# Sixteen additions a block that form the Strassen operands T1 to T4 at each change to gate and up: GpSimd instead of VectorE

## The chip, the cores and the metric

The kernel runs on one core of a Trainium2 chip. The time is that of the device in microseconds for one execution, the median of several runs. The engines of the core are TensorE (PE), VectorE (DVE), ScalarE (ACT), GpSimd (POOL) and SyncE (SP); DMAs are issued from the queues of SP, ACT and POOL.

## What is computed

Two residual steps on x of 8 x 256 x 1024 f32. The first adds a linear layer and a conditional difference with a matrix of signs; the second is a gated MLP of width 2752 with adapters of rank 16 picked per batch:

```python
sign = (2 * mask - 1).astype(x.dtype)
x = x + einsum('bsi,oi->bso', x, W) + b + einsum('bsi,bio->bso', x, sign) * coeff[:, None, None]

def lora_add(base, inp, A, B):                 # A, B picked by the batch's index
    t = einsum('bri,bni->bnr', A, inp)
    return base + einsum('bor,bnr->bno', B, t) * 0.5
gate = lora_add(x @ W_gate.T, x, A_gate, B_gate)
up   = lora_add(x @ W_up.T,   x, A_up,   B_up)
act  = silu(gate) * up
x = x + lora_add(act @ W_down.T, act, A_down, B_down)
```

## The kernel before

**Stages.** The eight batches are worked on in two blocks s of four, and a block in two halves of N = 512 columns. A first stage makes x1 (the result of the first step) for both blocks and stores it to `x1_scratch`; it ends at about 201 us. Then each block has its gate and up stage over 22 tiles f of the width, and its down stage. The order in which TensorE goes through the work is written out in `pe_order` (L99), and ScalarE and VectorE follow the same list of events.

**Precision.** Every operand of a matmul is split in a high part (a copy rounded to fp32r, made by ScalarE) and a low part (the operand less its high part, made by VectorE), and each product is three matmuls: high by high, high by low, low by high.

**Strassen.** Gate and up of tiles 1 to 20 are one 2x2 block product by a Strassen-Winograd form of seven products (`PRODUCTS`, L32). Beside the four parts B11, B21, B12 and B22 of x1 it needs T3 = B22 - B12, T2 = B11 + T3, a T1 made from B22 less T2, and T4 = B21 - T2, each for four k of 128 rows: sixteen additions of 128x512 f32 a block (`MADE`, L57). They are made in place in the staging tiles `fx` and `early_x`, in which the parts of x1 have been loaded by SyncE. `form_hi` (L827, ScalarE) and `form_lo` (L1179, VectorE) then round them into `op_b`.

**The order at a change of stage.** Tile 0 is worked by four plain products (events `h`, eight in each half), and between them stand the adapters' A products (events `ta`), which take small tiles `lw` that ScalarE and VectorE split shortly before (`lora_a`); then come the small adapter products `r` (0 and 1, with B_gu) and the Strassen products of tile 1, `g` 1: p1, p5, p6, then `r` 1, p3, p7, p2, the A_down product `td` 0, and p4. `first_tile_steps` (L68) says behind which event ScalarE and VectorE do which step: `a_part` splits adapter tiles, `forms` rounds an operand, `make` makes T3, T2 and T1 of one k, `make4` makes T4, `t sum`, `t own`, `t high` and `t low` treat the A product's result, `lora_b` rounds B_gu, `result` makes a = silu(gate) * up of tile 0. Both engines run these steps strictly in the written order. `form_hi` of T1 to T4 waits for the count `form_t` of makings; `form_make` (L1162) is VectorE's.

**Queues.** GpSimd only issues DMAs (L632 to L786). Behind the last store of x1 it issues the twelve loads of B_gu (`load_b_gu(adapter, 0)`, L723) and the four of A_down (L724). In the loop over blocks it waits until the last adapter tile of the second half is split (L727), issues eighteen loads of the next B_gu (L728) and then stores the operands for the down stage one by one (L740). In block 1 its B_gu and A_down loads have been issued in the down stage of block 0 (L783 to L786). SyncE loads T4's part B21 for k = 2 and 3 when T1 of that k has its low part (L561), since it takes the same staging tile.

Of the kernel before, what the change touches and what calls it, by code (L numbers as in the profile page):

```python
# [67 lines left out]
def first_tile_steps():  # L68

    def a_part(half, *firsts):  # L70
        return [("lw", half, o) for o in firsts]

    def forms(name, *ks):
        return [("form", name, k) for k in ks]

    return {("h", 0, 0): a_part(0, 0, 2) + forms("b12", 1, 2, 3, 0) + forms("b22", 0, 1),
            ("h", 0, 3): forms("b22", 2, 3),
            ("ta", 0, 1): a_part(0, 4) + [("make", 0)],
            ("ta", 0, 3): a_part(0, 6) + [("make", 1)] + forms("t1", 0),
            ("ta", 0, 5): a_part(1, 0) + [("make", 2)] + forms("t1", 1),  # L80
            ("ta", 0, 7): a_part(1, 2) + [("t sum", 0), ("make", 3)] + forms("t1", 2) + [("t own", 0)] + a_part(1, 4)
                          + [("t high", 0), ("t low", 0), ("lora_b", 0)] + forms("t1", 3),
            ("ta", 1, 1): forms("t2", 0, 1, 2, 3) + a_part(1, 6),
            ("r", 0): [("result", 0)],
            ("h", 1, 5): [("make4", 2), ("make4", 3)] + forms("t4", 2, 3),
            ("ta", 1, 7): [("t sum", 1)] + forms("t3", 0),
            ("g", 1, "p1"): [("t own", 1), ("t high", 1), ("t low", 1)] + forms("t3", 1),
            ("g", 1, "p5"): [("lora_b", 1)] + forms("t3", 2, 3) + [("make4", 0), ("make4", 1)],
            ("g", 1, "p6"): forms("t4", 0, 1),
            ("r", 1): [("result", 1)],  # L90
            ("g", 1, "p3"): [("second result",), ("t neg",)]}
# [119 lines left out]
def build(nc, x, mask, coeff, w0, bias, wgu, wgu_half, wd, wd_left, a_gu, a_down, b_gu, b_down, idx, ident, own,  # L211
# [13 lines left out]
    with ExitStack() as ctx:  # L225
# [238 lines left out]
        def lw_use(key):  # L464

            s = key[1]
            return s * (HALVES * KQ + FT) + (key[2] * KQ + key[3] // 2 if key[0] == "ta" else HALVES * KQ + key[2])
# [165 lines left out]
        def _(pool):  # L633
# [50 lines left out]
            def load_b_down(adapter, s, hp):  # L684
                if hp > 1:
                    pool.wait_ge(lo_ready, at["l", s, 2 * hp - 3] + 1)
                for q in range(2):
                    for b in range(4):
# [2 lines left out]
                                       b_down[ds(adapter[b], 1), :, 2 * P * hp:2 * P * (hp + 1)].rearrange(  # L691
                                           "a r n -> (a r) n")).then_inc(bd_loaded[hp % 2], 16)

            def load_operand(s, seg, u):
                name = MOVING[u]
                for kp in range(SEGK):
                    at_op = opd_at(seg, name, kp, 0)
                    pool.dma_start(op_d[:, at_op:at_op + 2, :].rearrange("p a n -> p (a n)"),  # L698
                                   ops_d[s, seg * SEGK + kp, STORED[name], :, :]
                                   ).then_inc(opd_loaded[opd_sem(seg, name, kp)], 16)  # L700
# [23 lines left out]
            load_a_down(adapter)  # L724
            for s in range(BLOCKS):

                pool.wait_ge(lw_l, lw_use(("ta", s, HALVES - 1, HT - 1)) + 1)  # L727
                load_b_gu(adapter, 1)  # L728
                for kp in range(KP):
# [400 lines left out]
        def _(dve):  # L1130
# [28 lines left out]
                cols = slice(h * N, (h + 1) * N)  # L1159
                sub(xs[s][:, 2 * k + 1, cols], src, xs[s][:, 2 * k, cols]).then_inc(xl_ready, 1)  # L1160

            def form_make(s, name, k):  # L1162
                out = fx_ap(later_cell(name, k))
                t2_ap = fx_ap(later_cell("t2", k))
                if name == "t3":
                    dve.wait_ge(form_l, form_count(s, "b22", k))
                    end = sub(out, fx_ap(STAGED["b22", k]), out)
                elif name == "t2":
                    dve.wait_ge(fx_loaded[STAGED["t2", k]], 16 * fx_turn[s, "later", "t2", k])
                    dve.wait_ge(form_t, made_count(s, "t3", k))  # L1170
                    end = add(out, fx_ap(later_cell("t3", k)), out)
                else:
                    if name == "t4":
                        dve.wait_ge(fx_loaded[STAGED["t4", k]], 16 * fx_turn[s, "later", "t4", k])
                    dve.wait_ge(form_t, made_count(s, "t2", k))
                    end = sub(out, out, t2_ap)
                end.then_inc(form_t, 1)

            def form_lo(s, name, k):  # L1179
                dve.wait_ge(form_h, form_count(s, name, k))  # L1180
                sub(op_b[:, op_at(name, k, 1), :], form_src(name, k), op_b[:, op_at(name, k, 0), :]).then_inc(form_l, 1)
# [91 lines left out]
            def first_result(s, half):  # L1273
                if half:
                    dve.wait_ge(form_l, form_count(s, "t3", KQ - 1))
                dve.wait_ge(pe_done, done["r", s, half])
                dve.wait_ge(silu_made, silu_count(s, 0, half))
                mult(a32[:, half, :], (g1, g2)[half][:, :], first_bank(1, half)[:, :]).then_inc(a_made, 1)
                operand_lo((s, 0, ("b11", "b12")[half]), a32[:, half, :])
                if half:  # L1280
                    dve.wait_ge(a_made, a_count(s, 0, 1))
                    sub(t_sum[:, :], a32[:, 1, :], a32[:, 0, :]).then_inc(tm, 1)
# [164 lines left out]
            for key in plan.events:  # L1447
# [17 lines left out]
                for kind, *args in steps_after.get((key[0], *key[2:]), ()):  # L1465
# [2 lines left out]
                        continue  # L1468
                    elif kind == "form":
                        form_lo(s, *args)  # L1470
                    elif kind == "make":
                        for name in ("t3", "t2", "t1"):
                            form_make(s, name, *args)
                    elif kind == "make4":
                        form_make(s, "t4", *args)
                    elif kind == "lw":
                        lora_a(("ta", s, *args))
                    elif kind == "lora_b":
# [290 lines left out]
```

## Time and profile before

| | |
|---|---|
| median of 3 runs | 1579.45 us (1579.41 to 1581.66) |
| span of the profiled execution | 1579.3 us |
| stretches with TensorE always busy | 262 to 660 us, for one |
| the two changes to gate and up | about 201 to 257 us and 889 to 946 us |
| granted TensorE clock, mean | 0.995 of full |
| DMA queues of GpSimd, of SyncE | 33.4% and 26.0% of the 16 DMA engines' span |

PE is the matmul part of TensorE, PEld its weight loads, which overlap; two matmuls that follow each other overlap in the records. A line of the timeline gives the start, the time to the end of the last of "x" instructions, and in brackets the idle time of the engine before it and what ended it. L1132, L1135 and L1138 are VectorE's helpers for subtracting, adding and multiplying, L791 is ScalarE's copy, L1509 and L1505 are TensorE's helpers, so the tile names tell what a step is.

### The profile page before, as it was taken

To read this page: it belongs to the slowest core of one execution; us is meant where nothing else is said; L and a number is where in the kernel's file an instruction comes from. 1 tells how busy PE (TensorE), PEld (TensorE's weight loads), DVE (VectorE), ACT (ScalarE), POOL (GpSimd) and SP (SyncE) were. 2 spreads that over 40 slices of the span, in tenths; PEclk is the share of its full clock that TensorE was granted. 3 is DMA by queue.
4 is the path that set the end of the run, shared out by engine and by line. 5 is a ranking of instruction groups with operands and counts; after the bars stand their busy time and mean duration, and the time that the engine had idled before them with its cause. 6 is when DMAs were issued, how large, how long until landed. Compare 5 with 4: busy or idle time off the path is not lost.

```text
span 1579.3 us, 23432 instructions
## 1 busy us (share of the span) xinstructions
PE 1545.1 (98%) x7550; PEld 1304.1 (83%) x7550; DVE 1220.1 (77%) x2136; ACT 802.3 (51%) x1478; POOL 426.1 (27%) x821
## 2 busy tenths in 40 slices
PE   6999998999999999999999989999999999999999
PEld 6999986888888888878888868888888888778887
DVE  8999887676666677688888887767766667798886
ACT  8999855444444444443334464444444444443332
POOL 0000142333333333253410024332323233443100
PEclk9999999999999999999999999999999999999999
DMA  9999854444444444699593725444444445996653
GB/s 372 374 361 376 322 172 127 147 137 154 144 139 155 156 157 153 230 334 312 168 375 111 241 78 168 157 139 134 148 152 148 131 157 179 316 374 220 216 196 116
DMA packets 141961, 325.66 MB, mean 206 GB/s; under 512 B 22416, under 2 KB 50320, under 8 KB 141840
## 3 DMA queue, kind: packets, MB, share of 16 engines
q0 software_dynamic: 61216, 176.21, 33.4%
q1 hardware_dynamic: 76016, 139.57, 26.0%
q10 hardware_dynamic: 4608, 8.39, 1.4%
q8 instruction: 61, 1.00, 0.3%
q14 instruction: 60, 0.49, 0.1%
HBM read 233.51 MB, written 90.18 MB: 205 GB/s over the span
## 4 chain that ended last, share of the span: by engine, by line
PE 87%; DVE 7%; issue 2%; ACT 2%; DMA 1%; SPq 1%; ACTq 0%; POOL 0%; DVEq 0%
PE ps L1509 59%; PE ps L1505 26%; PE ps L1645 2%; DVE m_raw L1135 1%; DVE m_lo L1132 1%; DVE op_b L1132 1%; DMA acc<-x_scratch 1%; DVE acc L1135 1%; DMA m_raw<-in_mask 1%; DVE lo L1132 1%; ACT hi L791 0%; DVE fx L1132 0%; SPq L512 0%; DVE raw L1132 0%; DVE act_t L1306 0%
## 5 line engine op out<-in xcount | busy, mean ns | idle before, releaser
L1509 PE MATMUL ps<-op_b,hi 128*128 128x512 f32 x1616 | 503.4, 393 | 9.3 <-DVE u L1135 5.6
L1132 DVE TENSOR_TENSOR lo<-raw,hi 128x512 fp32r<-128x512 f32 (+2 forms) x640 | 333.4, 530 | 128.7 <-ACT hi L791 126.7
L791 ACT ACTIVATE hi<-raw 128x512 fp32r<-128x512 f32 (+1 forms) x592 | 304.9, 519 | 220.9 <-PE ps L1509 182.9
L1509 PEld LDWEIGHTS ps<-op_b,hi 128*128 128x128 f32 x1616 | 306.0, 190 | 74.1 <-DVE u L1135 6.4
L1509 PE MATMUL ps<-op_b,lo 128*128 128x512 f32 x808 | 318.0, 394 | 0.0
L1509 PE MATMUL ps<-op_d,hi 128*128 128x512 f32 x800 | 248.5, 392 | 4.4 <-DVE acc L1135 4.1
L1505 PE MATMUL ps<-op_b,hi 128*128 128x512 f32 x816 | 252.0, 390 | 0.0
L638 POOL DMA_DIRECT2D operand_scratch<-ot x140 | 75.3, 541 | 552.4 <-DVE ot L1132 536.1
L1135 DVE TENSOR_TENSOR acc<-acc,ps 128x512 f32<-128x512 f32 x248 | 169.9, 685 | 51.0 <-PE ps L1509 43.3
L1509 PEld LDWEIGHTS ps<-op_d,hi 128*128 128x128 f32 x800 | 147.8, 188 | 39.8 <-DVE acc L1135 9.8
L1505 PEld LDWEIGHTS ps<-op_b,hi 128*128 128x128 f32 x816 | 153.4, 188 | 30.7
L1509 PEld LDWEIGHTS ps<-op_b,lo 128*128 128x128 f32 x808 | 153.5, 190 | 29.7
L1505 PE MATMUL ps<-op_b,lo 128*128 128x512 f32 x408 | 159.1, 390 | 0.0
L1509 PE MATMUL ps<-op_d,lo 128*128 128x512 f32 x400 | 156.2, 391 | 0.0
L1132 DVE TENSOR_TENSOR raw<-raw 128x512 f32<-128x512 f32 (+1 forms) x240 | 133.1, 555 | 6.3 <-DVE lo L1132 0.5
L659 POOL DMA_DIRECT2D b_in<-in_b_gu x240 | 118.6, 494 | 16.6 <-issue 6.3
L791 ACT ACTIVATE ot<-a 128x512 fp32r<-128x512 f32 x104 | 65.1, 626 | 100.2 <-DVE a L1138 56.9
L656 POOL DMA_DIRECT2D b_in<-in_b_gu x144 | 75.2, 522 | 136.2 <-DVE lw L1132 112.1
L1505 PE MATMUL ps<-xs,m_hi 128*128 128x256 f32 x512 | 95.8, 287 | 13.0 <-DVE m_lo L1132 10.6
L698 POOL DMA_DIRECT2D op_d<-operand_scratch x140 | 75.3, 587 | 97.6 <-PE ps L1505 73.3
L1505 PE MATMUL ps<-op_d,hi 128*128 128x512 f32 x320 | 98.7, 390 | 0.0
L1132 DVE TENSOR_TENSOR ot<-a,ot 128x512 fp32r<-128x512 f32 x104 | 71.6, 688 | 34.9 <-ACT ot L791 34.9
(130 smaller groups left out, 2315.9 us busy)
## 6 DMA issues: line engine op xcount, KB each, us to landing
operand_scratch<-ot POOLq DMA_DIRECT2D x140, 512.0 KB, 3.9
op_d<-operand_scratch POOLq DMA_DIRECT2D x140, 512.0 KB, 10.9
raw<-in_wgu SPq DMA_DIRECT2D x168, 256.0 KB, 3.8
m_raw<-in_mask SPq DMA_DIRECT2D x64, 512.0 KB, 5.9
raw<-in_wd SPq DMA_DIRECT2D x160, 128.0 KB, 4.7
w_in<-in_w SPq DMA_DIRECT2D x32, 512.0 KB, 6.7
x_scratch<-x_out POOLq DMA_DIRECT2D x32, 256.0 KB, 4.8
acc<-x_scratch POOLq DMA_DIRECT2D x16, 512.0 KB, 7.5
```

The lines of the kernel that those rows point to most:

```text
L638: pool.dma_start(ops_d[s, kp, STORED[name], :, :], ot[:, 2 * slot:2 * slot + 2, :].rearrange("p a n -> p (a n)")).then_inc(ot_stored[slot] ...
L656: pool.dma_start(tile[at_row[0], half, :, :], src).then_inc(b_loaded[c % 2], 16)
L659: pool.dma_start(tile[at_row[g], slot, g, :], src[:, g, :]).then_inc(b_loaded[c % 2], 16)
L698: pool.dma_start(op_d[:, at_op:at_op + 2, :].rearrange("p a n -> p (a n)"), ops_d[s, seg * SEGK + kp, STORED[name], :, :]).then_inc(opd_lo ...
L791: return nc.scalar.activation(o, i, ACT.Copy)
L1132: return nc.vector.tensor_tensor(o, a, b, ALU.subtract)
L1135: return nc.vector.tensor_tensor(o, a, b, ALU.add)
L1505: return mm(dst, weight, v, start=start, stop=stop)
L1509: return mm(dst, weight, v, start=False, stop=stop, skip_group_check=True)
L1645: end = mm(ps[6 + half][:, :], lw_ap(key, half), ot[:, i, :], start=f == 0 and i == slot, stop=False)
```

## The change

The four makings go to GpSimd. In each block it does all sixteen in the order of `MADE` (k by k: T3, T2, T1; then T4 of k = 2, 3, 0, 1) before it waits at L727 for the last adapter tile. The waits stay those of VectorE's version, and the steps `make` and `make4` leave `first_tile_steps`. VectorE gets one new wait, on the last making, before the second a of tile 0.

```diff
-            ("ta", 0, 1): a_part(0, 4) + [("make", 0)],
-            ("ta", 0, 3): a_part(0, 6) + [("make", 1)] + forms("t1", 0),
-            ("ta", 0, 5): a_part(1, 0) + [("make", 2)] + forms("t1", 1),
-            ("ta", 0, 7): a_part(1, 2) + [("t sum", 0), ("make", 3)] + forms("t1", 2) + [("t own", 0)] + a_part(1, 4)
+            ("ta", 0, 1): a_part(0, 4),
+            ("ta", 0, 3): a_part(0, 6) + forms("t1", 0),
+            ("ta", 0, 5): a_part(1, 0) + forms("t1", 1),
+            ("ta", 0, 7): a_part(1, 2) + [("t sum", 0)] + forms("t1", 2) + [("t own", 0)] + a_part(1, 4)
...
-            ("h", 1, 5): [("make4", 2), ("make4", 3)] + forms("t4", 2, 3),
+            ("h", 1, 5): forms("t4", 2, 3),
...
-            ("g", 1, "p5"): [("lora_b", 1)] + forms("t3", 2, 3) + [("make4", 0), ("make4", 1)],
+            ("g", 1, "p5"): [("lora_b", 1)] + forms("t3", 2, 3),
...
+            def form_make(s, name, k):
+                out = fx_ap(later_cell(name, k))
+                t2_ap = fx_ap(later_cell("t2", k))
+                if name == "t3":
+                    pool.wait_ge(form_l, form_count(s, "b22", k))
+                    end = nc.gpsimd.tensor_tensor(out, fx_ap(STAGED["b22", k]), out, ALU.subtract)
+                elif name == "t2":
+                    pool.wait_ge(fx_loaded[STAGED["t2", k]], 16 * fx_turn[s, "later", "t2", k])
+                    pool.wait_ge(form_t, made_count(s, "t3", k))
+                    end = nc.gpsimd.tensor_tensor(out, fx_ap(later_cell("t3", k)), out, ALU.add)
+                else:
+                    if name == "t4":
+                        pool.wait_ge(fx_loaded[STAGED["t4", k]], 16 * fx_turn[s, "later", "t4", k])
+                    pool.wait_ge(form_t, made_count(s, "t2", k))
+                    end = nc.gpsimd.tensor_tensor(out, out, t2_ap, ALU.subtract)
+                end.then_inc(form_t, 1)
...
             for s in range(BLOCKS):
 
+                for name, k in MADE:
+                    form_make(s, name, k)
                 pool.wait_ge(lw_l, lw_use(("ta", s, HALVES - 1, HT - 1)) + 1)
                 load_b_gu(adapter, 1)
...
                 if half:
                     dve.wait_ge(form_l, form_count(s, "t3", KQ - 1))
+                    dve.wait_ge(form_t, made_count(s, *MADE[-1]))
                 dve.wait_ge(pe_done, done["r", s, half])
```

## Rows read from the trace of the kernel before

**Rows 1.** The page: busy us, share of the span and instructions of each engine.
```profile
PE 1545.1 (98%) x7550; PEld 1304.1 (83%) x7550; DVE 1220.1 (77%) x2136; ACT 802.3 (51%) x1478; POOL 426.1 (27%) x821
```

**Rows 2.** Stretches: length, each engine's busy us, granted clock, DMA share, GB/s.
```profile
196.00:262.00 66.00, 58.96 (x269) 48.28 (x268) 53.62 (x91) 40.78 (x79) 20.12 (x39) 0.96 0.44 144
880.00:950.00 70.00, 63.49 (x262) 50.86 (x261) 58.48 (x99) 40.80 (x79) 10.17 (x20) 0.95 0.42 141
262.00:660.00 398.00, 398.00 (x1782) 329.81 (x1781) 276.65 (x455) 185.38 (x361) 125.83 (x246) 1.00 0.47 153
...
218.00:228.00 10.00, 10.00 (x46) 8.24 (x45) 9.59 (x18) 7.63 (x16) 0.48 (x2) 1.00 0.42 137
...
257.00:262.00 5.00, 4.63 (x11) 3.67 (x12) 4.11 (x7) 1.69 (x3) 1.08 (x2) 0.50 0.29 105
```

**Rows 3.** Timeline of TensorE's matmuls, both changes: start, us, what, idle before.
```profile
217.27 0.39 PE L1625 MATMUL ps<-op_b,lw 128*128 128x512 f32 x1
...
220.90 0.39 PE L1625 MATMUL ps<-op_b,lw 128*128 128x512 f32 x1
...
237.96 0.73 PE L1509 MATMUL ps<-op_b,hi 128*128 128x512 f32 x2 [1.43 <-ACT ps L791]
...
257.37 1.22 PE L1509 MATMUL ps<-op_b,hi 128*128 128x512 f32 x2 [3.12 <-DVE u L1135]
...
931.36 0.47 PE L1509 MATMUL ps<-t_gate,t_neg 96*128 96x512 f32 x1 [1.72 <-DVE t_up L1132]
...
946.01 1.22 PE L1509 MATMUL ps<-op_b,hi 128*128 128x512 f32 x2 [2.47 <-DVE u L1135]
```

**Rows 4.** The chain of waits in the two changes: start, us, what.
```profile
219.74 0.03 ACT lw L791
...
233.18 1.30 DVE fx L1132 x2
...
246.47 1.29 DVE early_x L1132 x2
...
893.66 4.91 DVE op_b L1132 x8
```

**Rows 5.** Instructions on the tile fx: ns min/median/max, first and last start.
```profile
L791 ACT ACTIVATE op_b<-fx x44: 614/617/635, 199.0 to 933.4; 128x512 fp32r<-128x512 f32 x44
...
L1132 DVE TENSOR_TENSOR fx<-fx x20: 670/685/693, 209.9 to 922.4; 128x512 f32<-128x512 f32 x20
```

**Rows 6.** Timeline of ScalarE, block 0.
```profile
218.75 0.91 ACT L921 ACTIVATE u<-g,own_sb 64x256 f32<-64x256 f32 x2 [0.77 <-DVE g L1135]
...
223.07 2.70 ACT L791 ACTIVATE op_b<-fx 128x512 fp32r<-128x512 f32 x5
...
233.90 1.23 ACT L791 ACTIVATE op_b<-fx 128x512 fp32r<-128x512 f32 x2 [1.36 <-DVE fx L1132]
```

**Rows 7.** Timeline of VectorE: the first two makings, T2 waits for T3.
```profile
209.86 0.69 DVE L1132 TENSOR_TENSOR fx<-fx 128x512 f32<-128x512 f32 x1
210.65 0.69 DVE L1135 TENSOR_TENSOR fx<-fx 128x512 f32<-128x512 f32 x1
```

**Rows 8.** Timeline of GpSimd, both changes.
```profile
209.36 6.63 POOL L656 DMA_DIRECT2D b_in<-in_b_gu  x12 [6.06 <-PE ps L1626]
216.11 2.33 POOL L681 DMA_DIRECT2D ad_in<-in_a_down  x4
227.97 0.53 POOL L656 DMA_DIRECT2D b_in<-in_b_gu  x1 [9.52 <-DVE lw L1132]
...
916.66 0.53 POOL L656 DMA_DIRECT2D b_in<-in_b_gu  x1 [102.61 <-DVE lw L1132]
```

**Rows 9.** The two loads of fx (T4's) in 219 to 236 us: us from issue to landing.
```profile
DMA to landing us min/median/max: 2.5/2.6/2.7
```

**Rows 10.** Timeline of ScalarE, block 1.
```profile
904.12 0.60 ACT L791 ACTIVATE u<-ps 64x512 f32<-64x512 f32 x1
...
907.57 0.91 ACT L921 ACTIVATE u<-g,own_sb 64x256 f32<-64x256 f32 x2 [0.76 <-DVE g L1135]
```

More of the change, by code:

```diff
@@ L1160, in x_lo @@
                 sub(xs[s][:, 2 * k + 1, cols], src, xs[s][:, 2 * k, cols]).then_inc(xl_ready, 1)
[L1162 to L1177, printed above, removed]
             def form_lo(s, name, k):
@@ L1470, in _ @@
                         form_lo(s, *args)
[L1471 to L1475, printed above, removed]
                     elif kind == "lw":
```

## The prediction

> **What bounds the kernel now.** I read the busy shares first [rows 1]: TensorE is busy for 1545.1 of 1579.3 us, so nearly all of the time is matmuls and only 34 us of the span can hold waits. The table by stretches says where [rows 2]: from 262 to 660 us TensorE is busy for 398.00 of 398.00 us, and VectorE's 276.65 us cost nothing there. The two changes from block to block, 196 to 262 and 880 to 950 us, hold the open places: 7.04 and 6.51 us without a matmul. TensorE's own timeline gives the waits and their releasers [rows 3]: in block 0 1.43 us before p6 and 3.12 before p4 (two shorter ones lie between), in block 1 1.72 before the second small adapter product and 2.47 before p4. What releases them is ScalarE or VectorE, never GpSimd. The chain of waits [rows 4] then shows which engine holds the way in between: in block 0 from 219.74 us ScalarE and VectorE in turns, in block 1 VectorE from 893.66 us. T-makings lie on it: two T4 at 233.18 (1.30 us), two T4 at 246.47 (1.29 us), and the same in block 1. So the change aims at work that is on the path. The question is what the same work costs on GpSimd, and from when GpSimd is free.
>
> **What is removed.** Thirty-two two-operand operations on 128x512 f32 leave VectorE, sixteen a block, at 0.685 us median [rows 5]. Back to back VectorE ends eight such in 4.91 us [rows 4], which makes 10 us a block, but most of it fills time in which it would wait anyway. On the path are the four T4. In block 0 ScalarE sits idle for 1.36 us before it can round T4 [rows 6]; with T4 made beforehand 1.28 of that goes (0.08 stays for its own waits). At 246.47 the two T4 hold VectorE itself: 1.29 us, 1.21 by the rate at which it starts them. That is 2.5 us a block. What is next late there is ScalarE's roundings and the product a (the elementwise product of gate and up) on VectorE, which both move up with it; TensorE has the 7.04 us of idle time to move into. For block 1 I take the same 2.5 us: TensorE's work between its waits at 931.36 and 946.01 stays below the chain of the other two by the 2.47 us at its end.
>
> **What one making costs on GpSimd.** The trace of before has no arithmetic of that size on GpSimd, only DMA issues and four one-element memsets, so I bound it. Below: it is as fast as on VectorE, where dependent makings follow each other every 0.79 us (209.86 to 210.65) [rows 7]. Above: GpSimd takes in the two operands one after the other, at the rate at which ScalarE, a one-input engine, passes 512 elements, 0.617 us [rows 5]: 1.24 us; 0.10 us from VectorE's row (0.79 less 0.69) for the semaphore to its own next instruction gives 1.34 us; and each of them waits for one VectorE instruction in flight, 0.69 us more: 2.03 us. I take p = 1.34 us. For the operation itself I go to the slower price because GpSimd's nearest rows, DMA issues of about 0.55 us each that move no tile at all [rows 8], are not those of a quick engine; as to collisions I go to the lower one, because VectorE has little to do while the makings run.
>
> The Trainium skill, page "GPSIMD Engine Reference", section "Performance versus the Vector engine", gives 1.96 times VectorE's time for a two-input add of 2048 elements. As an estimate from that page, 0.685 x 1.96 + 0.10 = 1.44 us, and by the formula below the whole would be 10.7 us instead of 8.9. No row of before shows it.
>
> **Block 0: where the new queue bites.** On VectorE the first making started at 209.86 us. On GpSimd it stands behind what that queue does first: twelve B_gu loads from 209.36 (6.63 us) and four A_down loads from 216.11 (2.33 us) [rows 8]. GpSimd is free at 218.44. In the order of MADE, T1 of k is ready at 218.44 + 3p(k+1): 222.5, 226.5, 230.5 and 234.5 us. ScalarE rounds T1 in the middle of its own fixed order, so what stands behind it waits too: behind T1(0) the adapter tile of the second half, which TensorE used at 217.27 [rows 3]. It comes at 222.46 + 0.54 (rounding) + 0.31 + 0.35 (the tile's two steps) = 223.7, so TensorE stands for a new 6.4 us there. That is not yet the sum, because the later ones are worse. Behind T1(2) stands "t own", at 218.75 now [rows 6] and on the path right after it. It would start at 218.44 + 9p + 0.55 = 231.05. The lag is 9p + 0.24, less 0.08 us that ScalarE waits for TensorE at 219.74: 12.2 us. TensorE goes from one of these tiles to the next in 3.63 us (217.27 to 220.90) [rows 3] against 3p = 4.0, so it isn't what is late. T1(3) comes 3p = 4.0 us after T1(2) and is wanted 4.9 us after it (0.55 + 223.07 - 218.75) [rows 6]; it costs nothing while p is below 1.62. T4(2) and T4(3) need their loads, which wait for T1's low parts and land 2.6 us after issue [rows 9]: some 4 us ahead of ScalarE's need for the first, about even for the second. Block 0: 12.2 - 2.5 = **9.7 us later**.
>
> **Block 1: the queue is empty.** GpSimd has waited 102.61 us when it issues its next load at 916.66 [rows 8], so the makings start when B22(0) has its low part. That is the fifth of the eight that start at 893.66 and take 4.91 us [rows 4]: 893.66 + 5 x 0.61 = 896.7. T1(2) is ready at 896.7 + 9p, "t own" starts at 896.7 + 12.06 + 0.55 = 909.3 against 907.57 [rows 10]: 1.74 us late, less 2.5 us: **0.8 us earlier**. If p were small, "t own" could not start before ScalarE's copy at 904.12 [rows 10] (0.60) and VectorE's sum (0.69), 905.4, so at most 2.15 us would be won at this place.
>
> **Moved behind the makings.** The eighteen B_gu loads that start at 227.97 and 916.66 [rows 8] and the first operand store wait for T4(1). In block 0 it is done about two p after the load of T4(3) has landed, some 6 us (in the time of before) behind the old start. Eighteen at about 0.55 us take 10 us. Their users, the rounding of tile 2's B_gu and an ot slot that is wanted again, stand behind p4 or close before it, whose wait ends at 257.37 [rows 3]. I cost this at nothing; if that cover were gone it would be up to 6 us a block. The new wait of VectorE on the last making, before the second a, holds nothing: T4(1) is ready over 10 us before. The SyncE queue only gains from an earlier T1 and loses from a later one, which is in the lag.
>
> **The sum.** 9p + 0.16 - 2.5 for block 0 and 9p - 10.3 - 2.5 for block 1: 18p - 15.2 us in round figures. With p = 1.34 this is 24.1 - 15.2 = 8.9 us. The profiled execution has a span of 1579.3 us and the runs a median of 1579.45, so the two agree; 1579.45 + 8.9 = **1588.4 us**. TensorE runs at half clock after long idling (0.50 granted in 257 to 262, behind the 3.12 us) [rows 2]. A new 6.4 us stop brings one more such stretch, 2 us of extra matmul time, but TensorE has that much spare before r(0), where the other engines' lag is larger; nothing is added.
>
> **The rivals.** (1) **The two engines block each other.** VectorE's and GpSimd's operations read the same tiles at the same time, and if one waits out the other each time, p is 2.03: 36.5 - 15.2 = 21.3 us, and T1(3) binds as well (3 x 2.03 - 4.9 = 1.2 us a block): 1603 us. For it speaks that VectorE is busy for 9.59 of 10 us in 218 to 228 [rows 2]; against, that five of those instructions leave it and that in block 0 the rest wait for the makings, so that VectorE stands idle while GpSimd works. The Trainium skill, page "SBUF — State Buffer", section "Who interferes with whom", has this as a rule: a VectorE instruction with two SBUF inputs and a GpSimd instruction that reads SBUF exclude one another for a whole instruction. By that rule the makings and VectorE's low parts would take turns; no row of before shows it. Chance 0.09.
> (2) **GpSimd is as quick as VectorE.** p = 0.79: block 0 is 7.3 - 2.5 = 4.8 us later, block 1 2.15 + 2.5 = 4.65 us earlier; 0.2 us together, 1579.6 us. Up to p = 1.02 the result would stay within 3.2 us. For it: the elements and lanes are the same. Chance 0.07.
> (3) **The open places swallow block 0's lag (faster).** If what releases TensorE at its four waits from p6 to p4 did not hang on "t own" but on its own earlier work, the 7.04 us there would take the lag up. With p = 0.79, 7.3 - 7.04 = 0.3 us remain in block 0 and block 1 gains 4.65: 1575.1 us. It decides from p below 0.95. Against it: the chain of waits runs from 219.74 to 257.37 without a piece that doesn't hang on the one before. Chance 0.04.
>
> **How the numbers follow.** Forecast 0.80, rivals 0.09, 0.07 and 0.04. The forecast's own range is p from 1.0 (2.8 us) to 1.85 (18.1 us, between 1.34 and the full collision): 1582.5 to 1598 us. It leaves out the three rivals. 0.2% of this time is 3.2 us, about what a measurement of this kernel can tell from no change. Slower by more: the forecast but its lowest edge, and rival 1: 0.88. Within: rival 2 and that edge: 0.08. Faster: 0.04.
>
> **What would show it.** In the changed profile: the first making on GpSimd at 218.4 us in block 0 and 896.7 in block 1; groups of three every 4.0 us; TensorE idle at 217.3 for over 6 us and again before the small adapter product; ScalarE waiting for GpSimd's fx before each T1 in block 0 and hardly for T4; TensorE's wait before p4 ending 9.7 us later in block 0, and the distance from it to the same place of block 1, 688.6 us now, shorter by 0.8 us. Wrong would be the forecast if a making takes under 1.0 us, if GpSimd starts earlier than its loads end, or if the time of VectorE's low parts rises beside the makings.

## The result: 1599.8 us, 1.3% slower, and the profile after

The changed kernel takes a median of 1599.82 us (1598.21 to 1601.54, four runs) against 1580.17 for the kernel before beside it: ratio 1.0126, 95% interval 1.0114 to 1.0139. That is 19.7 us lost where 8.9 us had been forecast. The direction was right; the time lies above the range. The profiled execution has a span of 1599.7 us against 1579.3 (20.4 us more).

The page's busy shares first, which answer [rows 1]; then two stretches that hold the changes to gate and up (columns as in [rows 2]):

```profile
PE 1550.2 (97%) x7550; PEld 1306.8 (82%) x7550; DVE 1222.9 (76%) x2104; ACT 801.6 (50%) x1478; POOL 476.2 (30%) x853
...
196.00:280.00 84.00, 64.45 (x279) 51.69 (x278) 52.95 (x75) 40.13 (x79) 43.80 (x55) 0.88 0.35 122
895.00:965.00 70.00, 62.80 (x258) 49.82 (x256) 58.02 (x78) 37.87 (x76) 34.88 (x35) 0.95 0.40 138
```

VectorE has 32 instructions fewer and is busy 2.8 us *longer* than before (1222.9 against 1220.1). That alone says that its other instructions have grown by some 25 us: 32 at 0.685 us, 22 us, have gone. In the first stretch TensorE is without a matmul for 19.6 of 84 us. Its own timeline names the waits (block 0, then block 1; the answer to [rows 3]):

```profile
229.00 0.80 PE L1623 MATMUL ps<-op_b,lw 128*128 128x512 f32 x1 [10.71 <-DVE lw L1151]
241.74 0.50 PE L1507 MATMUL ps<-t_gate,t_neg 96*128 96x512 f32 x1 [2.06 <-DVE t_neg L1151]
...
275.31 0.94 PE L1507 MATMUL ps<-op_b,hi 128*128 128x512 f32 x2 [2.85 <-DVE u L1154]
...
932.82 0.50 PE L1507 MATMUL ps<-t_gate,t_neg 96*128 96x512 f32 x1 [3.43 <-DVE t_neg L1151]
966.38 0.73 PE L1507 MATMUL ps<-op_b,hi 128*128 128x512 f32 x2 [2.88 <-DVE u L1154]
```

The lines 275.31 and 966.38 are p4 of the two blocks. What VectorE's tile at the first wait was itself late for stands in GpSimd's timeline (the answer to [rows 8]; block 0, then the first making of block 1):

```profile
205.54 0.54 POOL L731 DMA_DIRECT2D x_scratch<-x_out  x1 [7.34 <-ACT x_out L843]
212.70 6.63 POOL L656 DMA_DIRECT2D b_in<-in_b_gu  x12 [6.61 <-PE ps L1624]
219.45 2.33 POOL L681 DMA_DIRECT2D ad_in<-in_a_down  x4
221.88 1.28 POOL L699 TENSOR_TENSOR fx<-fx 128x512 f32<-128x512 f32 x1
223.31 1.26 POOL L703 TENSOR_TENSOR fx<-fx 128x512 f32<-128x512 f32 x1
224.64 1.26 POOL L708 TENSOR_TENSOR fx<-fx 128x512 f32<-128x512 f32 x1
...
237.46 2.97 POOL L708 TENSOR_TENSOR fx<-fx 128x512 f32<-128x512 f32 x2
245.09 2.89 POOL L708 TENSOR_TENSOR fx<-fx 128x512 f32<-128x512 f32 x1 [4.66 <-DMA fx<-x_scratch]
247.94 3.42 POOL L708 TENSOR_TENSOR early_x<-early_x,fx 128x512 f32<-128x512 f32 x2
...
911.57 1.66 POOL L699 TENSOR_TENSOR fx<-fx 128x512 f32<-128x512 f32 x1 [80.92 <-DVE op_b L1151]
```

One making takes 1.26 to 1.29 us alone, and the first three follow each other every 1.33 us, as forecast (1.34). In block 0 they begin right behind the sixteen adapter loads, again as forecast. Two things were not: the loads themselves begin at 212.70 us, not 209.36, and VectorE's timeline beside the makings looks like this (adapter tiles `lw`, a low part of T1, the adapter's results, the weight sums `raw` of tile 1, and in block 1 the eight low parts):

```profile
212.77 0.29 DVE L1151 TENSOR_TENSOR lw<-a_in,lw 128x128 fp32r<-128x128 f32 x1 [1.97 <-ACT lw L810]
231.86 1.36 DVE L1151 TENSOR_TENSOR lw<-a_in,lw 128x128 fp32r<-128x128 f32 x1
233.14 0.67 DVE L1154 TENSOR_TENSOR g<-ps,u 64x512 f32<-64x512 f32 x1
235.13 1.10 DVE L1151 TENSOR_TENSOR op_b<-fx,op_b 128x512 fp32r<-128x512 f32 x1 [1.31 <-ACT op_b L810]
236.15 1.38 DVE L1151 TENSOR_TENSOR lw<-a_in,lw 128x128 fp32r<-128x128 f32 x1
237.56 1.73 DVE L1151 TENSOR_TENSOR t_gate<-u,t_gate 32x512 fp32r<-32x512 f32 x1
...
241.00 0.68 DVE L1151 TENSOR_TENSOR t_neg<-b_in,t_neg 32x512 fp32r<-32x512 f32 x1
...
244.94 0.68 DVE L1154 TENSOR_TENSOR raw<-raw 128x512 f32<-128x512 f32 x1
...
246.14 0.68 DVE L1151 TENSOR_TENSOR lo<-raw,hi 128x512 fp32r<-128x512 f32 x1
246.93 3.29 DVE L1151 TENSOR_TENSOR raw<-raw 128x512 f32<-128x512 f32 x2
250.15 1.76 DVE L1151 TENSOR_TENSOR lo<-raw,hi 128x512 fp32r<-128x512 f32 x1
...
908.38 7.09 DVE L1151 TENSOR_TENSOR op_b<-fx,op_b 128x512 fp32r<-128x512 f32 x8 [0.23 <-ACT op_b L810]
```

The same small tile `lw` takes 0.29 us while GpSimd issues DMAs and 1.36 to 1.38 us while it adds: 1.09 us more, most of one making. `t_gate` takes 1.73 beside a making and `t_neg`, started 0.6 us after GpSimd's pair (237.46 + 2.97) ended, its usual 0.68. And one VectorE instruction is *not* held up in the midst of the makings: `g<-ps,u` at 233.14, 0.67 us, beside the making at 233.15. Its one operand is in PSUM (`ps`), so only one is read from SBUF; all those that grow read two from SBUF. The eight low parts of block 1 take 7.09 us, 4.91 in [rows 4].

GpSimd can be the one that waits. T4(3) starts at 245.09 us, just behind the first of three VectorE instructions without a gap (244.94 to 246.82). They keep their 0.68 us each, and the making takes 2.89 us: it ends 1.16 us after the last of them, about one making. Behind that both engines have work without a gap and take turns: the two makings at 247.94 need 1.71 us each, and each `raw` about 1.6.

The chain of waits shows both parts in order of time: GpSimd's loads, its makings, and then ScalarE and VectorE with the lengthened pieces.

```profile
221.24 0.54 POOL ad_in L681
221.88 1.29 POOL fx L699
...
233.15 1.29 POOL fx L708
234.47 0.64 ACT op_b L810
235.13 1.10 DVE op_b L1151
```

**The account.** I take TensorE's first adapter product of block 0 as the zero, since it lies ahead of everything that the change touches: 208.20 us before, 209.06 after. From there to p4 it is 49.17 us before (257.37) and 66.25 after: **17.1 us lost in block 0**. "t own" stands at 25.94 us instead of 10.55, +15.4; from it to the low part of `t_neg` 4.51 us become 6.00, +1.5; from there to the product a (251.83) 7.87 become 10.83, +3.0, all of it in `raw` and `lo` (1.42 and 0.69 us before); from a to p4 26.24 become 23.48, -2.8, the relief. 15.4 + 1.5 + 3.0 - 2.8 = 17.1. **Block 1**, from the eight low parts (893.66, 908.38) to p4: 52.35 us become 58.00, 5.7 lost: "t own" +3.8, then +1.65, +3.0, -2.8. Between p4 of block 0 and those low parts 3.2 us come back (636.29 us before, 633.07 after), of which more below, and 0.9 us lie ahead of the zero: 0.9 + 17.1 + 5.7 - 3.2 = 20.5 against 20.4 in the spans; from p4 of block 1 to the end it is 633.3 us in both. These are two single profiles. A second one of the kernel before (below) has 49.16 us in block 0, but 53.16 in block 1, so block 0's loss stands and block 1's is 4.8 to 5.7 us. The difference is in "t own", 14.57 us behind the low parts there and 13.91 in the first profile.

### The profile page after: what moved, and what is told of

It reads as the page before. It is cut to its first block, busy times and chain, and to the rows that moved or that the text cites. A ratio compares the mean times of both kernels' runs of the same rounds, so it can differ in the third digit from the quotient of the medians.

```text
span 1599.7 us, 23436 instructions
## 1 busy us (share of the span) xinstructions
PE 1550.2 (97%) x7550; PEld 1306.8 (82%) x7550; DVE 1222.9 (76%) x2104; ACT 801.6 (50%) x1478; POOL 476.2 (30%) x853
## 4 chain that ended last, share of the span: by engine, by line
PE 89%; DVE 4%; POOL 2%; issue 2%; ACT 1%; DMA 1%; SPq 0%; ACTq 0%; POOLq 0%; DVEq 0%
PE ps L1507 60%; PE ps L1503 27%; PE ps L1643 2%; DVE op_b L1151 1%; DVE lo L1151 1%; POOL fx L703 1%; DVE acc L1154 1%; POOL fx L708 1%; POOL fx L699 1%; ACT hi L810 0%; DMA acc<-x_scratch 0%; DMA x_first<-in_x 0%; DVE raw L1151 0%; DVE t_up L1151 0%; ACT op_b L810 0%
## 5 line engine op out<-in xcount | busy, mean ns | idle before, releaser
L1151 DVE TENSOR_TENSOR raw<-raw 128x512 f32<-128x512 f32 (+1 forms) x240 | 136.9, 570 | 6.2 <-DVE lo L1151 0.5
L659 POOL DMA_DIRECT2D b_in<-in_b_gu x240 | 118.8, 496 | 13.9 <-issue 5.0
L1503 PE MATMUL ps<-xs,m_hi 128*128 128x256 f32 x512 | 96.3, 288 | 12.8 <-DVE m_lo L1151 11.4
L1507 PE MATMUL ps<-xs,m_hi 128*128 128x256 f32 x512 | 95.3, 287 | 0.0
```

The lines of the kernel that those rows point to most:

```text
L659: pool.dma_start(tile[at_row[g], slot, g, :], src[:, g, :]).then_inc(b_loaded[c % 2], 16)
L1151: return nc.vector.tensor_tensor(o, a, b, ALU.subtract)
L1503: return mm(dst, weight, v, start=start, stop=stop)
L1507: return mm(dst, weight, v, start=False, stop=stop, skip_group_check=True)
```

## The experiments

My theory after this reading: (a) a late start behind GpSimd's own queue in block 0, and (b) GpSimd's additions and VectorE's instructions with two SBUF operands shut each other out, which costs VectorE most, against (c) a relief of 2.8 us a block from T4. Rivals: the price of GpSimd's instructions alone, or the start alone.

**One block at a time.** Both kernels hold both versions of `form_make` and choose by block (a part of the edit, against the changed kernel; the three other lines with makings get them back likewise, and VectorE skips those that GpSimd does):

```diff
+def on_gpsimd(s, name, k):
+    return s == 0        # blk1: s == 1
...
-            ("ta", 0, 1): a_part(0, 4),
+            ("ta", 0, 1): a_part(0, 4) + [("make", 0)],
...
                 for name, k in MADE:
-                    form_make(s, name, k)
+                    if on_gpsimd(s, name, k):
+                        form_make(s, name, k)
```

> Makings on GpSimd in block 0 only; block 1 keeps them on VectorE. Theory A (GpSimd starts late in block 0, behind its sixteen loads, and then its reads and VectorE's two-operand instructions hold each other up): the wait before p4 of block 0 ends 14 to 15 us later than before, as in the changed kernel, and the total is 11.5 to 14.5 us over before, because some 1.4 to 3 us are given back at a fixed place after it. Theory B (collisions only, a late start costs nothing of its own): both blocks cost the same, about 6 us here. Rival C (block 1 carries the loss): under 5 us here.

Measured: 1596.4 us, ratio 1.0102 (1.0085 to 1.0119), +16.2 us. p4 of block 0 comes 14.3 us later against TensorE's first adapter product (63.48 us), as expected; the total is 1.7 us above the range. In its profile the surplus stands behind p4 of block 1 (957.92 us), where the code is that of the kernel before: 637.8 us to the end instead of 633.3. Its cause is open.

> Makings on GpSimd in block 1 only. GpSimd has been idle for 80 us there, so no late start. Theory A: from the start of the eight low parts to the wait before p4 block 1 is 5.7 us longer than before; total 3 to 6 us over before. If a late start were all (theory Q), block 1 would cost nothing or win 0.8 us, as forecast.

Measured: 1584.59 us, ratio 1.0023 (1.0013 to 1.0033), +4.4 us. The two add up to 20.6 us against 19.7 for both. Block 1, where GpSimd's queue is empty, still loses, and its profile (of the kernel with block 1 alone) shows the low parts held up as in the changed kernel:

```profile
891.34 3.10 DVE L1157 TENSOR_TENSOR op_b<-fx,op_b 128x512 fp32r<-128x512 f32 x5 [0.23 <-ACT op_b L816]
...
949.29 1.07 PE L1537 MATMUL ps<-op_b,hi 128*128 128x512 f32 x2 [2.85 <-DVE u L1160]
```

The first five of the eight low parts go at their usual rate (3.10 us), since nothing is ready for GpSimd until the fifth, B22(0), is done; the three behind it take the rest of 7.10 us. p4 comes 57.95 us after 891.34, 5.6 more than in the first profile of the kernel before, 4.8 more than in the second.

**The late start alone.** VectorE makes everything as before, but its first making waits until the twelve B_gu loads have landed:

```diff
             def form_make(s, name, k):
                 ...
+                    if (s, k) == (0, 0):
+                        dve.wait_ge(b_loaded[0], 16 * 12)
```

> All makings stay on VectorE; only the first of block 0 waits until the twelve B_gu loads have landed, about when GpSimd would get free (some 8 us late), and the GpSimd queue does no arithmetic. Measures the late start by itself. Theory A: T1(2) is 8.7 us late, nothing collides, no relief: 8 to 9 us over before, in block 0 alone, and VectorE's adapter tiles stay at 0.28 us. Theory B: under 3 us.

Measured: 1589.38 us, ratio 1.006 (1.0044 to 1.0077), +9.2 us. Against TensorE's first adapter product (208.88) the first making starts at 11.29 us instead of 1.66 and p4 (267.67) stands at 58.79 instead of 49.17: 9.6 us later in, 9.6 us later out. So a late making in block 0 is handed on in full, and no instruction of VectorE is longer than before. In the changed kernel the first making starts 12.82 us after that product, 11.2 later than before. By the same rule that is 11.2 of block 0's 17.1 us. From the first making to "t own" it loses another 4.2 us (13.12 instead of 8.89), the price of GpSimd's makings and the collisions in between. So the start alone isn't enough.

**No late start.** The changed kernel with nine makings ahead of the B_gu loads, three between them and the A_down loads, T4 behind:

```diff
+            for name, k in MADE[:9]:
+                form_make(0, name, k)
...
             load_b_gu(adapter, 0)
+            for name, k in MADE[9:12]:
+                form_make(0, name, k)
             load_a_down(adapter)
...
-                for name, k in MADE:
+                for name, k in MADE[12:] if s == 0 else MADE:
```

> The changed kernel, but in block 0 the first nine makings stand ahead of the B_gu loads, three between them and the A_down loads, the T4 behind those. Theory A: T1(2) ready near 218.5 us (as on VectorE), but then the B_gu loads come 5 us later than the small adapter product wants them and the collisions stay: block 0 costs 5 to 8 us instead of 14.6, total 8 to 12 us over before. If a late start were all (Q): about 3 to 4 us over before. Theory B (collisions only): no gain on the changed kernel, 19 us over before.

Measured: 1592.95 us, ratio 1.0086 (1.0069 to 1.0103), +12.8 us, above the 8 to 12 expected. It wins 6.9 us of 19.7; block 0 still costs 10.4 us (p4 59.55 us after TensorE's first adapter product), not 5 to 8. VectorE's timeline shows why not more: the makings now meet the low parts of B as well, and B_gu comes late instead.

```profile
205.09 5.90 DVE L1155 TENSOR_TENSOR op_b<-fx,op_b 128x512 fp32r<-128x512 f32 x6 [0.22 <-ACT op_b L814]
...
229.38 1.02 DVE L1155 TENSOR_TENSOR t_neg<-b_in,t_neg 32x512 fp32r<-32x512 f32 x1 [3.52 <-ACT t_neg L814]
```

Six low parts take 5.90 us, 3.70 before; `t_neg` waits 3.52 us for ScalarE, which waits for B_gu.

**What shuts VectorE out: writes, one read, two reads.** Two kernels keep order and waits of the changed kernel and replace each making. T1 to T4 have other values in both, so part of the result is left out.

```diff
-                    end = nc.gpsimd.tensor_tensor(out, fx_ap(later_cell("t3", k)), out, ALU.add)
+                    end = nc.gpsimd.memset(out, 0.0)                              # memset
+                    end = nc.gpsimd.tensor_scalar(out, out, 2.0, None, ALU.mult)  # oneread
```

> The changed kernel with each of GpSimd's sixteen makings a block replaced by a memset of the same tile (same waits, same places): it writes 128x512 and reads nothing, so T1 to T4 are left out as values. Theory A1 (it is GpSimd's reading that holds VectorE's two-operand instructions up): VectorE's adapter tiles between the makings are back at 0.28 us from 1.35 and the roundings at 0.68 from 1.1 us, the eight low parts of block 1 take 4.9 us again, not 7.1; the late start of block 0 stays. Rival A2 (any SBUF traffic of GpSimd does it): they stay longer wherever a memset runs beside them.

Measured: 1581.85 us, ratio 1.0005 (0.9996 to 1.0015). With GpSimd only writing, 0.53 us each, nothing on VectorE is longer than before. Its timeline where VectorE's two-operand instructions run beside the memsets:

```profile
220.71 0.54 POOL L699 MEMSET fx<- 128x512 f32 x1
...
223.17 0.69 DVE L1151 TENSOR_TENSOR op_b<-fx,op_b 128x512 fp32r<-128x512 f32 x1 [11.02 <-ACT op_b L810]
223.78 0.28 DVE L1151 TENSOR_TENSOR lw<-a_in,lw 128x128 fp32r<-128x128 f32 x1
...
236.29 0.99 POOL L708 MEMSET early_x<- 128x512 f32 x2
236.70 0.68 DVE L1151 TENSOR_TENSOR lo<-raw,hi 128x512 fp32r<-128x512 f32 x1
```

The late start is still there: p4 stands at 262.93, 54.79 us after TensorE's first adapter product instead of 49.17. It comes back in what follows: TensorE runs at full clock behind that p4 (0.50 in [rows 2]), from it to the low parts of block 1 it is 631.3 us (633.7 and 636.3 in two profiles of the kernel before), and from these to p4 50.42 instead of 52.35, block 1's relief without a collision (946.01 us and the end of the program are 633.3 us apart before, 635.1 here, so 1.8 us go again).

> The changed kernel with each making replaced by a multiplication of the tile by 2 in place: one operand read instead of two, the same amount written; T1 to T4 are left out as values. A1: VectorE's adapter tiles between them are still held up, by up to the length of one such instruction. If only GpSimd's second operand did it, they would be back at 0.28 us. The length of one against 1.28 us for two operands also tests the price that was worked out (1.24 = two passes of 0.617): 0.62 to 0.75 us by that.

Measured: 1597.08 us, ratio 1.0102 (1.0085 to 1.012). The instruction that reads one operand takes 1.49 us, longer than the addition of two (1.29), where 0.62 to 0.75 had been expected. So my price from "two passes of 0.617" had the right size for a wrong reason. On VectorE it holds up much less:

```profile
219.64 1.52 POOL L699 TENSOR_SCALAR fx<-fx 128x512 f32<-128x512 f32 x1
...
230.35 0.29 DVE L1151 TENSOR_TENSOR lw<-a_in,lw 128x128 fp32r<-128x128 f32 x1
235.42 0.67 DVE L1151 TENSOR_TENSOR lw<-a_in,lw 128x128 fp32r<-128x128 f32 x1 [0.31 <-ACT lw L810]
238.59 1.14 DVE L1151 TENSOR_TENSOR t_neg<-b_in,t_neg 32x512 fp32r<-32x512 f32 x1
...
246.53 1.10 DVE L1151 TENSOR_TENSOR lo<-raw,hi 128x512 fp32r<-128x512 f32 x1
```

So the hold-up grows with what GpSimd reads from SBUF: none for a write, 0 to 0.5 us for one operand, 0.4 to 1.1 us for two, and 2.5 where two additions follow each other. The operations differ in kind too, not only in operands, so which property of them matters isn't separated. GpSimd still waits: one of its instructions beside three of VectorE without a gap takes 3.16 us. The total is nearly that of the changed kernel because nine instructions of 1.49 us make T1 later still. Block 1, with no late start, shows the collisions in time as well: from its low parts to p4 it is 54.93 us with these longer instructions and 58.00 with the additions. So the price of GpSimd's instructions alone isn't what costs there.

**GpSimd's start.** The kernel with block 0 alone had its B_gu loads start 0.75 us after TensorE's first adapter product (209.82, 209.07), the changed kernel 3.64 us (212.70, 209.06); its p4 stood at 63.48 us, the other's at 66.25. The loads wait for the last store of x1 to land, although they don't use it. So I moved them ahead of that wait:

```diff
             pool.wait_ge(pe_done, last_s)
+            load_b_gu(adapter, 0)
+            load_a_down(adapter)
             for i in range(X1_RING):
                 pool.wait_ge(x1_stored[i], 16 * x1_store_counts(BLOCKS - 1)[i])
-            load_b_gu(adapter, 0)
-            load_a_down(adapter)
```

> The changed kernel with one edit in GpSimd's queue: the twelve B_gu and four A_down loads are issued ahead of the wait for the last stores of x1 instead of behind it. Results are not changed by this. Theory A: everything from 'T1(2)' to p4 of block 0 hangs on the moment at which GpSimd's queue is free. In the changed kernel the B_gu loads start at 212.70 us, 6.6 us behind the issue of the last store (205.54 + 0.54), because they wait for its landing. Without that they start at about 206.1, the makings at 215.3 instead of 221.88, 't own' at about 228.2 instead of 235.0, and p4 of block 0 comes some 6.5 us earlier: about 1593.3 us, or 1593 to 1594 with TensorE's clock. Block 1 is as in the changed kernel. It would also explain why the kernel with the makings on GpSimd in block 0 alone, whose loads happened to start 0.75 us behind TensorE's first adapter product instead of 3.64, had its p4 2.8 us earlier against that product than the changed kernel. Theory B: the collisions with VectorE set the pace, or what T4 waits for (its loads, the ring of tiles): then the makings start earlier but p4 gains less than 3 us: 1597 us or above.

Measured: 1592.4 us, ratio 1.0072 (1.0055 to 1.0088), +11.4 us: 7.4 us under the changed kernel's median, 8.2 when each is taken against the kernel before beside it.

```profile
204.86 6.63 POOL L656 DMA_DIRECT2D b_in<-in_b_gu  x12 [0.51 <-issue]
...
214.04 1.30 POOL L699 TENSOR_TENSOR fx<-fx 128x512 f32<-128x512 f32 x1
...
239.15 3.30 DVE L1151 TENSOR_TENSOR raw<-raw 128x512 f32<-128x512 f32 x2
...
267.53 0.92 PE L1507 MATMUL ps<-op_b,hi 128*128 128x512 f32 x2 [2.82 <-DVE u L1154]
```

The makings start at 214.04 instead of 221.88 (7.84 us earlier), p4 at 267.53 instead of 275.31 (7.78 earlier), and the distance from p4 of block 0 to p4 of block 1 (958.60) is 691.07 us, to the hundredth that of the changed kernel. Theory A holds. The collisions are all still there (`raw` 3.30 us), and their cost on the path is a constant on top.

**T4 on GpSimd alone.** The relief is real and needs neither the late start nor T1 to T3. In the kernel before, T4(0) and T4(1) go to GpSimd behind its eighteen B_gu loads and first store:

```diff
+            def make_t4(s, k):
+                pool.wait_ge(fx_loaded[STAGED["t4", k]], 16 * fx_turn[s, "later", "t4", k])
+                pool.wait_ge(form_t, made_count(s, "t2", k))
+                out = fx_ap(later_cell("t4", k))
+                nc.gpsimd.tensor_tensor(out, out, fx_ap(later_cell("t2", k)), ALU.subtract).then_inc(form_4, 1)
...
+                        if kp == 0 and name == "b11":
+                            for k in LATE_T4:        # (0, 1)
+                                make_t4(s, k)
```

> The kernel before with only T4(0) and T4(1) on GpSimd, behind the eighteen B_gu loads and the first operand store, where VectorE waits for ScalarE anyway. Theory A: the relief without the late start and with at most one collision: the stretch from the product a to p4 about 1.2 us shorter in each block less 0 to 0.5 us of collision, 1.5 to 2.4 us under before in all. If the relief of T4 were not real (rival R: something else is late there), no change.

Measured: 1576.08 us, ratio 0.9973 (0.9962 to 0.9984), by that ratio 4.3 us faster than the kernel before and more than the 1.5 to 2.4 expected.

```profile
238.72 2.56 POOL L699 TENSOR_TENSOR early_x<-early_x,fx 128x512 f32<-128x512 f32 x2
...
238.67 3.17 DVE L1145 TENSOR_TENSOR lo<-raw,hi 128x512 fp32r<-128x512 f32 x1 [0.23 <-ACT hi L801]
...
256.51 1.22 PE L1524 MATMUL ps<-op_b,hi 128*128 128x512 f32 x2 [2.55 <-DVE u L1148]
```

Even here a single `lo` that meets the two makings takes 3.17 us instead of 0.69, but it stands where VectorE had room.

> The kernel before with all four T4 on GpSimd, in the order of k, ahead of the eighteen B_gu loads. Theory A: relief of 2.7 us a block from the product a on, but T4(0) and T4(1) of block 0 run from 218.4 us beside VectorE's makings on the path, and T4(2) and T4(3) beside the low parts and the weight sums: 1 to 1.3 us for each that collides, so between 2 us under and 3 us over before. Rival R: 2 us or more over before.

(All four T4, ahead of the B_gu loads for the next tiles: `LATE_T4 = (0, 1, 2, 3)` at the place of the loop's start.) Measured: 1580.84 us, ratio 1.0004 (0.9995 to 1.0013). T4(0) and T4(1) of block 0 meet a making on VectorE's path, and T4(2) and T4(3) VectorE's low parts (in block 1 as well, 5.28 us for five, 3.10 without company):

```profile
218.45 3.43 DVE L1144 TENSOR_TENSOR fx<-fx 128x512 f32<-128x512 f32 x1
...
226.38 5.28 DVE L1144 TENSOR_TENSOR op_b<-fx,op_b 128x512 fp32r<-128x512 f32 x5
```

What the four free is eaten. From TensorE's first adapter product to p4 of block 0 it is 51.17 us, 2.0 more than before, and in block 1 54.45, 1.3 to 2.1 more. That the total is no longer fits TensorE's clock, which was granted at 0.999 of full in the mean of this profile and at 0.995 and 0.996 in two of the kernel before; it isn't worked out further.

**The same two kernels again.** Is the gain of 4.3 us more than chance?

> The kernel before, unchanged, looked at a second time, as the yardstick for the gain of 4.3 us where T4(0) and T4(1) alone are on GpSimd. In the two profiles that gain is 1.0 us up to p4 of block 0 (256.51 - 209.54 = 46.97 us from the first B_gu load instead of 257.37 - 209.36 = 48.01) and 3.25 us from there to the eight low parts of block 1 (633.04 instead of 636.29), where neither kernel differs from the other in its code. Theory A, the 3.25 us follow from the shorter wait before p4: TensorE at half clock until 259.4 us instead of 262.1, worth some 1.4 us, and the rest from ScalarE's stores. Then this run shows again about 48.0 and about 636, with half clock past p4 for some 5 us and ScalarE's store issue of 2.33 us longer than 0.34 each. Theory B, the 3.25 us are a chance of that one execution: then this run gives a distance nearer to 633 for the same code. The time is that of the kernel before within 0.2% under both.

Measured: 1579.42 us, ratio 0.9997 (0.9988 to 1.0006).

> T4(0) and T4(1) alone on GpSimd, the same code as in the run before with that change, once more on this chip beside the kernel before. If its gain of 4.3 us (ratio 0.9973, 0.9962 to 0.9984) is real, this ratio lies within 0.996 to 0.9985. If the part of it that stands behind p4 (3.25 us of it in one execution) was chance, the ratio is near 0.9994 (only the 1.0 us up to p4 of block 0). In the profile: p4 of block 0 some 47.0 us behind the first B_gu load, VectorE's lo beside the two makings about 3.2 us instead of 1.4 for two, half clock behind p4 for about 3 us, and the eight low parts of block 1 some 633 us behind p4.

Measured: 1575.69 us, ratio 0.9971 (0.9959 to 0.9983). The gain is real. From TensorE's first adapter product to p4 of block 0 it is 49.17 and 49.16 us in the two profiles of the kernel before and 48.11 and 48.10 in the two with T4(0) and T4(1) on GpSimd: 1.06 us. From there to the low parts of block 1 the kernel before shows 636.29 and 633.68 us for the same code, the other 633.04 and 631.97. So 3.25 us in the first comparison become 1.71 in the second, and about half of what the first showed behind p4 was chance, the second theory: the same code differs by 2.6 us there, and three of ScalarE's store issues by 1.8.

```profile
889.29 3.20 ACTq L954 DMA_DIRECT2D out<-acc  x3
...
888.61 1.41 ACTq L954 DMA_DIRECT2D out<-acc  x3
```

(The first line is from the profile before, the second from its repeat.) Behind p4 the granted clock is 0.50 until 262 us in both profiles of the kernel before, until about 259 in one with T4 moved and never in the other, where TensorE had waited only 0.90 us. The mean granted clocks of the single runs point the same way. Of the eight of the first series with T4 moved, the two with a mean granted clock of 0.996 took 1580.5 and 1578.6 us, the six with 0.997 to 0.999 1574.1 to 1576.2; the kernel before mostly has 0.996. But one run of the second series took 1576.3 us at 0.996. So only 1.06 us of the gain has a place in block 0 that both pairs of profiles show, some of the rest is the clock, and I can't split it further.

## Why the prediction was off

**Right.** The bound and the place. The price of one making without company (1.34 forecast, 1.33 us measured from one to the next). The queue: first making right behind the sixteen loads, 9.18 us after their start against 9.08. The order in which the lag travels: T1(2), then "t own", then all of it to p4; what was costed at nothing (the B_gu loads behind the makings, VectorE's new wait) ends none of TensorE's waits. The relief: 2.5 forecast, 2.8 measured. TensorE's stop behind 217 us is where it was forecast, but 10.7 us long instead of 6.4: 2.5 by the later start, and 1.8 because the small tile behind T1(0) has its low part 3.0 us after T1(0) and not 1.2. T4(3) waited 4.66 us for its load, so T4(1) was ready only at 251.4 us (247.94 + 3.42). VectorE's new wait stands before the second a, at 268.75 us, and held nothing, as forecast. But the last three makings came to stand beside `raw` and `lo`. Whether an earlier load would have saved the 3.0 us there was not tried; the low parts just ahead of them would have met the makings instead.

**Wrong, step 1: where GpSimd is free.** "GpSimd is free at 218.44" was taken from one profile in which the loads started 1.16 us after TensorE's first adapter product. They wait for a store of x1 to land, and nothing in the kernel before hangs on when that is: its second profile has them at 212.18 us, 3.83 us after that product, with p4 at the same place. In the changed kernel every us of it is on the path. In the profiled execution it was 3.64 us, 2.5 more than I had reckoned with. The four spans of the changed kernel (1599.7, 1596.5, 1596.6, 1599.9) fall into pairs 3.2 us apart, which would fit a start of either kind; that was only argued, since one of them has a profile. That the start is passed on in full is shown (7.84 us in, 7.78 out).

**Wrong, step 2: what a collision costs, and whom.** I asked only how much longer GpSimd's additions get (p up to 2.03) and took the low end "because VectorE has little to do while the makings run". GpSimd's side was nearly right in block 0 (nine makings in 12.55 us, 12.06 forecast). In block 1, where they start beside the low parts, nine take 13.93 us (911.57 to 925.50), a p of 1.55: 1.9 us that the sum lacks. VectorE's side had no term at all: small tiles of 0.28 us become 1.36, `t_gate` and `t_up` 1.7, the two weight sums and a low part 5.0 instead of 2.1. VectorE is indeed idle at first (busy for 2.3 of the 10.7 us of TensorE's stop), but the few instructions that it has there are the path. This is 1.5 + 3.0 us in block 0 and 1.65 + 3.0 in block 1. To the latter come 2.05 us by which "t own" lags more than forecast (3.8 against 1.74), 1.9 of them from p; against the second profile of the kernel before the lag is 3.1. The last sign that the prediction named against itself, longer low parts beside the makings, is there: 7.09 us instead of 4.91. The rule of the Trainium skill, page "SBUF — State Buffer", section "Who interferes with whom", that I had put down as a rival with a chance of 0.09, is what happened; the traces agree with it for two-operand additions on both sides, for a memset nothing is held up, and the instruction with one operand in PSUM isn't held up either. My rival let it work through p alone and arrived near the measured time by another sum.

**The terms.** Block 0: 9.7 forecast + 2.5 (start) + 0.7 (T1(2) 0.1 us later behind the loads' start and 0.6 in the makings and roundings) + 1.5 + 3.0 - 0.3 (relief) = 17.1 measured. Block 1: -0.8 forecast + 2.05 + 1.65 + 3.0 - 0.3 = 5.6, measured 5.7 against the first profile of the kernel before. The sign of block 1 was wrong: a queue that is free doesn't make the work free. Of the 3.2 us that come back between the blocks, 1.8 are as much as the store issues above, and against the second profile of the kernel before only 0.6 come back; so most of it belongs to the first profile and not to the change.

## What to carry to other kernels

When work moves to GpSimd, price both engines: list each VectorE instruction with two SBUF operands that will run beside it and lies on the path, and add to each what it may wait for a GpSimd instruction: 0.4 to 1.1 us here beside one of 1.27, more where two follow each other. GpSimd's own price grows as well where VectorE works without a gap. Check when the new engine's queue is free in more than one execution, since a start that nothing hung on before isn't steady. Move only those operations that fall where VectorE has slack and that the path needs soon after: two T4 of sixteen makings a block gave 4 us, of which 1.06 could be placed, and all sixteen cost 20.

## What the runs showed of the hardware

- GpSimd, 128x512 f32 in SBUF: addition of two tiles 1.26 to 1.29 us, multiplication of one tile by a constant in place 1.49, memset 0.53. The operation with one operand less isn't the faster one.
- VectorE beside GpSimd's additions: 128x128 with two SBUF operands 0.28 us before and up to 1.38, 32x512 0.68 and up to 1.73, 128x512 0.68 and 1.10 to 1.78. Beside two additions without a gap between them one 128x512 took 3.17 us, another 3.43. Beside GpSimd's one-operand instruction the 128x128 took 0.28 to 0.67. Beside memset, or with one operand in PSUM (0.67): no change.
- GpSimd's additions grow too, from 1.27 to 1.55 and up to 1.76, and to 2.89 and 3.04 beside three VectorE instructions without a gap, which themselves keep 0.68. Where both engines have work without a gap, one turn of both takes 1.71 us. The closest starts of each alone, 0.60 and 1.22 us, add up to 1.82, so they come close to taking turns by whole instructions; an instruction that grows by less has met the other one in the middle of its time.
